# A perceiver layer on one core: cross-attention re-tiled to one batch at a time, in three rounds of up to six token tiles, by pairs of heads

## The reference, cut to what matters

```python
# layer norms, cross-attention, self-attention, feed-forward with product-key experts
x = x + xattn(ctx, layernorm(x), mask, ...)      # this part is rebuilt
x = x + attn(layernorm(x), qw, kw, vw, ow)       # unchanged
x = x + ffn(layernorm(x), ...)                   # unchanged

def xattn(x, latents, mask, ...):                # x: 2 x 2048 x 512, latents: 2 x 128 x 512
    xn, lat = layer_norm(x, g1, b1), layer_norm(latents, g2, b2)
    q = lat @ Wq                                 # 16 heads of 64
    k, v = split(concat([xn, lat], 1) @ Wkv, 2)  # 2048 + 128 tokens
    w = softmax(mask(q k^T / 8))
    return (w @ v) @ Wout
```

## Time and profile before

| | us |
|---|---|
| median of 3 runs | 1060.95 (1060.92 to 1061.44) |
| the profiled execution | 1060.34 |
| its span | 1058.5 |

### The profile page before, as it was taken

The page is one execution under the profiler, slowest core; times in us unless marked ns, Lnnn a source line. Parts: engine busy times, 40 slices in busy tenths (PEclk is TensorE's granted clock), DMA queues, the critical chain, the costliest instruction groups (busy, mean ns, idle before and its releaser), DMA issues.

```text
span 1058.5 us, 17551 instructions
## 1 busy us (share of the span) xinstructions
PE 929.5 (88%) x6017; PEld 823.2 (78%) x6017; DVE 684.6 (65%) x1488; ACT 523.8 (49%) x1082; POOL 391.5 (37%) x533
## 2 busy tenths in 40 slices
PE   3576899999989999989999999999796686777996
PEld 2476788988978988978988989989674486666775
DVE  4756365656556656555666566566677569997886
ACT  5343546545536545536546546454437344344552
POOL 6423214215214215214225224142463446663342
PEclk9898699999989999999999999999897888989999
DMA  6220111211211201211211212103420413321220
GB/s 259 63 46 16 53 31 31 73 21 39 65 23 31 73 20 39 65 23 31 73 20 41 66 21 47 55 21 80 179 99 21 152 62 120 120 80 59 100 81 21
DMA packets 35689, 66.70 MB, mean 63 GB/s; under 512 B 4192, under 2 KB 7440, under 8 KB 34960
## 3 DMA queue, kind: packets, MB, share of 16 engines
q1 hardware_dynamic: 22992, 46.64, 12.5%
q0 software_dynamic: 12608, 18.88, 8.8%
HBM read 46.11 MB, written 0.52 MB: 44 GB/s over the span
## 4 chain that ended last, share of the span: by engine, by line
PE 47%; DVE 26%; ACT 12%; issue 10%; POOL 3%; DMA 1%; DVEq 0%; SPq 0%; ACTq 0%; POOLq 0%
PE pJ L1303 9%; PE pJ L1305 9%; PE pJ L1304 9%; PE pV L1377 7%; PE pT L1361 3%; DVE work L953 3%; ACT KV L636 3%; ACT PT L651 3%; PE pS L1398 2%; DVE tail L1282 2%; PE pS L1399 2%; DVE st L969 2%; DVE KV L867 2%; DVE KLO L867 1%; PE pX L1415 1%
## 5 line engine op out<-in xcount | busy, mean ns | idle before, releaser
L867 DVE TENSOR_TENSOR PT<-pT,PT 128x512 fp32r<-128x512 f32 (+1 forms) x160 | 97.7, 611 | 248.0 <-ACT PT L651 247.8
L666 ACT ACTIVATE work<-work,negm 128x512 f32<-128x512 f32 (+1 forms) x160 | 105.5, 660 | 270.5 <-DVE negm L957 270.5
L1377 PE MATMUL pV<-KV,PT 128*128 128x128 f32 x1088 | 155.6, 283 | 16.7 <-DVE O L936 8.9
L1303 PE MATMUL pJ<-W,XA 128*128 128x256 f32 (+1 forms) x552 | 160.1, 290 | 5.3 <-DVE KLO L867 5.3
L1305 PE MATMUL pJ<-W,XA 128*128 128x256 f32 (+1 forms) x552 | 157.5, 285 | 0.0
L1304 PE MATMUL pJ<-W,XA 128*128 128x256 f32 (+1 forms) x552 | 157.3, 285 | 0.0
L1377 PEld LDWEIGHTS pV<-KV,PT 128*128 128x128 f32 x1088 | 136.6, 195 | 21.4 <-DVE PT L867 21.1
L636 ACT ACTIVATE KV<-pJ 64x512 fp32r<-64x512 f32 (+3 forms) x216 | 122.0, 565 | 58.3 <-PE pJ L1305 56.2
L468 POOL DMA_DIRECT2D KV<-KV x144 | 77.4, 543 | 140.4 <-ACT KV L636 137.1
L1303 PEld LDWEIGHTS pJ<-W,XA 128*128 128x128 f32 x552 | 105.8, 192 | 15.4 <-DVE KLO L867 13.3
L1303 PE MATMUL pJ<-XA,W 128*128 128x512 f32 (+1 forms) x288 | 113.3, 393 | 3.2 <-DVE QL L867 1.8
(11 more groups left out here) (313 smaller groups left out, 2037.7 us busy)
## 6 DMA issues: line engine op xcount, KB each, us to landing
KV<-KV POOLq DMA_DIRECT2D x128, 128.0 KB, 2.5
raw<-in_ctx SPq DMA_DIRECT2D x8, 1024.0 KB, 5.2
wst<-in_L_ffn_Wg SPq DMA_DIRECT2D x4, 1024.0 KB, 6.4
raw<-in_L_ffn_Wu SPq DMA_DIRECT2D x4, 1024.0 KB, 5.1
work<-in_L_ffn_Wd SPq DMA_DIRECT2D x4, 1024.0 KB, 5.0
raw<-in_L_ffn_down_embed SPq DMA_DIRECT2D x8, 512.0 KB, 3.3
work<-in_L_ffn_up_embed SPq DMA_DIRECT2D x4, 1024.0 KB, 5.2
XS<-in_L_xattn_Wkv SPq DMA_DIRECT2D x2, 1024.0 KB, 9.8
```

Of the source, the lines that this page charges most:

```text
L666: ac.activation(SP[:, t % 2, 0:w], SP[:, t % 2, 0:w], ACT.Exp, bias=negm[:, par, i:i + 1], scale=XSC, accum_out=rs[:, par, i:i + 1]).then_ ...
L867: return ve.tensor_tensor(dst, src, hi.bitcast(F32), ALU.subtract)
L1303: te.matmul(dst, a(HI), b(HI), start=start, stop=False)
L1377: last = te.matmul(pVh[:, i, :, :], PT[:, t % 2, s, P * n:P * n + P], VT[:, par, :, b if first else n, DH * i:DH * i + DH], start=n == 0 a ...
```

## The change

Cross-attention takes one batch after the other, each in three rounds of 6, 6 and 5 token tiles (the latent tile is in the first). A round goes by pairs of heads: 2 x 3 x 8 = 48 iterations `I`, all written out, with no hardware loop. An iteration on PE has, in this order: the keys of the next pair for the first three tiles (12 matmuls of 384 columns), transposes of the probabilities of head 0, keys for the other tiles, scores of the next pair for the first half, outputs of head 0, rows of scales, transposes of head 1, a tile of values of the next group, scores for the second half, another tile of values, outputs of head 1, and in every second iteration two more tiles of values. The new sizes: keys 960 matmuls of 384 columns and 192 of 256; values 1632 of 256 as before; scores 480 of 384 and 96 of 256; outputs 544 of 256.

```diff
-                    te.matmul(pS[:, t % 2, 0:w], QT[:, QHL, h, cols], KHH[:, par, i // 2, i % 2, n], start=True, stop=False)
-                    te.matmul(pS[:, t % 2, 0:w], QT[:, QZ, h, cols], KLO[:, par, i // 2, n], start=False, stop=True).then_inc(s_qk, 1)
+                for o, (qs, ks) in enumerate(((HI, HI), (LO, HI), (HI, LO))):
+                    for h, rows in enumerate(ROWS):
+                        last = te.matmul(pS[:, h, 0:w], Q[rows, qs, p, :], KT[rows, q, ks, 0:w], start=o == 0, stop=o == 2)
...
-                    for n in range(tiles):
-                        for s in (HI, LO):
-                            last = te.matmul(pVh[:, i, :, :], PT[:, t % 2, s, P * n:P * n + P],
-                                             VT[:, par, :, b if first else n, DH * i:DH * i + DH],
+                    for i in range(n):
+                        last = te.matmul(pO[:, h, :, :], VT[:, G % 2, 3 * q + i, 2 * (I % 2) + h, :, :], PT[:, t % 3, :, P * i:P * i + P],
+                                         start=q == 0 and i == 0, stop=q == 1 and i == n - 1)
...
+            def rows_of_scales(I):
+                if R % SPLITS == 1:
+                    pe.wait_ge(c_alpha, m + 1)
+                else:
+                    pe.wait_ge(c_beta, pair_index(I) + 1)
+                for h in range(2):
+                    scale = (alpha if R % SPLITS == 1 else beta)[:, par, h:h + 1]
+                    last = te.transpose(pX[:, L * h:L * h + L], scale.broadcast_to([P, P]), ident[:, :])
+                    if R % SPLITS == SPLITS - 1:
+                        last = te.transpose(pX[:, 256 + L * h:256 + L * h + L], linv[:, par, h:h + 1].broadcast_to([P, P]), ident[:, :])
...
+            def finals(I):
+                ve.reciprocal(linv[:, par, :], lsum[:, cols]).then_inc(c_rec, 1)
+                ve.tensor_tensor(beta[:, par, :], alpha[:, par, :], linv[:, par, :], ALU.mult).then_inc(c_beta, 1)
+            def merge(I, h):
+                ve.tensor_reduce(Otmp[:, h, :], parts, AX.X, ALU.add).then_inc(c_red, 1)
+                row = ve.tensor_tensor(acc, acc, scl[:, 0, h, :], ALU.mult)
+                ve.tensor_tensor(Otmp[:, h, :], Otmp[:, h, :], scl[:, 1, h, :], ALU.mult).then_inc(c_mg, 1)
+            def join(I):
+                ve.tensor_tensor(OS[0:DH, :], OF[0:DH, par, 0, :], Omv[0:DH, :], ALU.add)
+                ve.tensor_tensor(OS[DH:P, :], OF[DH:P, par, 1, :], Omv[DH:P, :], ALU.add).then_inc(c_os, 1)
...
+            dve.wait_ge(c_o, 4 * ITERS)
+            dve.wait_ge(c_ol, 2 * PAIRS)
+            for b in range(B):
+                last = ve.memset(KV[:, 4096 * b:4096 * b + 4096].bitcast(U32), 0)
```

More of the change, by code:

```diff
@@ L685, in _ @@
[L685 to L691 removed]
+                last.then_inc(c_lh, 1)
+            for k in range(KD):
+                x_hi(0, k)
+            wv_hi(0)
+            query_hi(0)
+            key_hi(0, 0)
+            wk_hi(1)
+            for k in range(KD):
+                x_hi(1, k)
+            value_hi(0, 0)
+            key_hi(0, 1)
@@ new lines, in project_keys @@
+            def project_keys(n, q):
+                C, w = 2 * (n // PAIRS) + q, P * tiles(n // PAIRS, q)
+                bank = job_bank(f"K{n}.{q}")
+                if q == 0 and n > 0:
+                    pe.wait_ge(c_wkl, n)
+                elif q == 0:
+                    pe.wait_ge(c_w0, 2)
+                if n % PAIRS == 0:
+                    x_ready(C)
+                for k in range(KD):
+                    last = product(bank[:, 0:w], lambda s: WK[:, n % 2, s, k, :], lambda s: XT[:, C % 4, s, k, 0:w], k == 0, k == KD - 1)
+                last.then_inc(c_j, 1)
@@ new lines, in _ @@
+            for k in range(KD):
+                x_turn(0, k)
+            queries(0)
+            project_keys(0, 0)
+            scores(0, 0)
+            for t in value_tiles(0, 0):
+                project_value(0, 0, t)
+            for k in range(KD):
+                x_turn(1, k)
+            project_keys(0, 1)
+            scores(0, 1)
+            for i in (1, 2):
+                for t in value_tiles(0, i):
+                    project_value(0, i, t)
+            queries(1)
+            nb = [0]
@@ new lines, in transpose_rows @@
+            def transpose_rows(src, b, ready, count, c0=0):
+                pe.wait_ge(ready, count)
+                if nb[0] >= 2:
+                    pe.wait_ge(s_tl, nb[0] - 1)
+                for c in range(4):
+                    last = te.transpose(pT[:, nb[0] % 2, P * c:P * c + P], src[:, b, P * (c0 + c):P * (c0 + c) + P], ident[:, :])
+                last.then_inc(s_tt, 1)
+                nb[0] += 1
+            pe.wait_ge(c_ol, 2 * PAIRS)
+            for n in range(2):
+                last = rows(pS[:, 1, :], OT, 1, n, 4 * n, n == 0, n == 1)
+                last.then_inc(s_wuse, 1)
```

1371 lines of the change are left out of this document (795 added, 576 removed).

## The result

The changed kernel takes **1067.7 us** (median of 4 runs, 1065.8 to 1068.0), the kernel before 1060.9 (1060.2 to 1061.4): ratio 1.0057, 95% interval 1.0041 to 1.0073, so 0.6% slower. The forecast was 1039, 2% faster. The profiled execution took 1068.0 us with a span of 1066.2.

What follows compares the result with a forecast made beforehand. PE was taken to bound. Loop: 65 + (632.6 + 11.5 + 5.5 - 19) + 41 waits = 736.6; with 13.5 end, residual at 750.1 instead of 772.2, -22 from 1060.3: 1038.3, median 1039; range 1005 to 1080.

Steps and rivals of the forecast that it cites:

- halves of the array that run one after the other: Second rival: a scores call at 1.41 us, total 1078; chance 0.25 together with the other slower rival and the like.
- Outputs at 0.12, keys at 0.175: PE, cross-attention: us per output matmul (-50.3 in all) and per 384-column key matmul (keys +2.8 in all).
- Scores at 1.0 a call: PE, 96 calls of six score matmuls on two row halves, two form switches included: 96.0 against 73.0, +23.0 us.
- the first rival: Score pairs really run side by side, a call at 0.53 to 0.64 us: total 1009 us; chance 0.17.
- Start 65, end 13.5: First iteration's keys at 65 us (55 to 75); 13.5 us from last output matmul to residual, both memsets on the path.
- hide behind the statistics or cost that: End: POOL's splits of the next two blocks come 2 to 3 us later than the memsets, hidden or costing that.
- Beta, 1.6 x 16 = 26: Third rounds: PE waits ahead of the rows of scales, as DVE makes beta behind two maxima; 26 us.
- ACT after the exponentials, 15: Loop: scores wait for the next keys' high part, queued late on ACT, in 12 of 48 iterations; 15 us.
- the added ACT and POOL work on the weights (...) is hidden: Loop: PE still bounds at 13.8 us an iteration, against ACT 9.4 and POOL about 7.
- Third rival, DVE beside POOL: Third rounds: DVE's two-SBUF-operand instructions slow beside POOL, 15.9 us an iteration, total 1074; chance 0.25 with the second rival.
- The signs named: Residual at 750; wrong if six-tile iterations exceed 15 us or next blocks' loads delay the last small DMAs over 5.

Runs made afterwards that it cites:

- the swap of two lines: Changed kernel with x_lo (low part of a context block) put ahead of wv_lo in POOL's queue: 1041.4 us, ratio 0.9813.
- the filler run: Changed kernel with 38 unused identity transposes on PE ahead of each of the five waits at changes of round: 1057.1 us, ratio 0.9955.
- the sums beside it on DVE: Changed kernel with finals (linv, beta) earlier in DVE's queue and the third rounds' two sums moved from POOL to DVE: 1046.1 us, ratio 0.9858.
- the comparison with ACT's: Changed kernel with the third rounds' sums and beta on ACT, only the reciprocal on DVE, early: 1036.3 us, ratio 0.9753.

## Why the prediction was wrong, point by point

The forecast said 2% faster, and the kernel was 0.6% slower; 1067.7 lies between the stated 1005 and 1080, but the upper part of that range stood for halves of the array that run one after the other, and this did not come.

- **Outputs at 0.12, keys at 0.175.** Right: 0.120 and 0.174. The Trainium skill's rule ("TensorE: Matmul & The Clock Gate", Back-to-back issue gap), 162.5 ns for 384 columns, is 11 ns too low here; keeping to the rows was right. That section gives the rule for the isolated gap, which the prediction did not say, and about 131 ns a matmul for a sustained stream of 512 columns; the rows, at 230, are far from that too.
- **Scores at 1.0 a call.** Mis-sized, the first rival's mechanism held: 0.81 with the switches. Each switch costs 0.09, half of what I took (with the 0.11 behind the first matmul the two come to 0.28 instead of 0.36), and the six weight loads don't bound. Worth 20 us to the good. The drain of which the Trainium skill speaks ("TensorEngine Tiling (Array Packing)", Key Properties) would show as such a loss at a change of form; it is 0.28 us a call here and does not eat the gain. The first rival's time was still wrong by 60 us.
- **Start 65, end 13.5.** Right: 65.4 and 14.3. The memsets were on the path as told. But I wrote that POOL's splits "hide behind the statistics or cost that", and did not lay the two paths side by side: they end within 0.57 us of each other, so at this place neither gains more than that alone. What both together are worth stays open.
- **Beta, 1.6 x 16 = 26.** Right in its sum (28.7) by luck, wrong in its cause. The mechanism I named gives 0.6 to 0.9 us in eight iterations; the other seven, 1.7 to 4.8 us, are POOL's queue. The prediction had no wait for POOL's sums; it had counted POOL as busy for 7 of 13.8 us.
- **ACT after the exponentials, 15.** Too high, 3.3: ACT was busy for 7.9 us in an iteration of six tiles, not 9.4, and the scores waited for it in three iterations, not twelve.
- **The step that failed: "the added ACT and POOL work on the weights (...) is hidden".** It was a sum of busy time. An engine half busy still keeps its order, and `wv_lo` waits for ACT in the middle of it, with the block that the next round starts on, and the sums, queued behind. I asked what is queued behind a waiting instruction for DVE's and PE's waits, and not for `wv_lo` on POOL. It cost 22.6 us at the changes of round, which the swap of two lines showed. That the swap brings the time to 1041, so near the 1039 of the forecast, is luck: the scores (20 us) and ACT (12) that I had too dear make up for the clock and the small gaps.
- **No term for the clock in the loop.** Before, rounds 1 to 3 lost 3.4 us in 476 us to the lower clock, and I took that for the rule. I added waits and priced them at their length. In the loop 18.6 us went to it, behind waits of 2 to 5 us; the filler run shows for the five waits at the changes of round that this is a cost of its own.
- **Third rival, DVE beside POOL.** It did not come where I put it (the merges' multiplies took 0.28 to 0.30 on average), but on the two-column instruction for beta, which PE waits for (1.0 us in 7 of 16 iterations, 0.16 to 0.28 in the others). With the sums beside it on DVE it came to 11 us, by the comparison with ACT's. And DVE was busy for 8.7 us in an iteration of a third round, not 11.7.
- **The signs named.** Iterations of six tiles took 14.4 us (115.4 a round), under the 15 set as limit; the last small DMAs took 1.84 us and were not held up. The residual at 777 instead of 750 was the sign that fired.

Left open: the 10.6 us in gaps under 0.3 us in the loop, and the 2.7 us that the phases behind the residual took more (the stretches at the lower clock there are 57 us long, 50 before; that this is the cause was not tested).

## What to carry to other kernels

Busy shares tell whether an engine can bound, not whether it is in time: for each instruction that a queue stops at, list what stands behind it and who needs that next, above all at the turns of the outer loop. A wait of PE can cost more than its length: the five of 4.4 to 4.8 us cost half as much again in slower matmuls, and of the three waits of 2.0 us in the changed kernel two stood at the start of a stretch at the lower clock and one did not. If such a wait can't be removed, filling it with matmuls of no use already gains. Small steps between engines on the critical path belong where neither another queue's backlog nor POOL's reads can hold them; here ACT.

## What the runs showed of the hardware

- **Halves of the array take their matmuls in their own order.** With head 0's three matmuls ahead of head 1's three in the program, the records show the pairs 10 ns apart, and a call is as long as in alternation. The Trainium skill ("TensorE: Matmul & The Clock Gate", Part 3: Packing small matmuls) says that matmuls keep strict program order at start and end; by that, a call in turn would have been longer. The measurement decides: at least with two row halves they don't, and that an engine runs its instructions in the order of the program holds on PE only within a half. A record does not hold its place in the program; that the order reached the engine as written is taken from the code and from the 10 ns that were 3 before.
- **The tiled form costs 0.09 us on the way in, 0.11 behind its first matmul and 0.09 on the way out**, at 384 columns and full clock; with both heads on one half the 0.11 and the 0.09 behind are the same (starts at 0, 0.281, 0.456, and 0.265 behind the last).
- **A DVE instruction on 2 columns takes up to 1.2 us beside POOL**, as long as POOL's own instruction of two operands needs to end; with one SBUF operand it takes its 0.17, and beside POOL's TENSOR_SCALAR five of six took 0.15 to 0.16.
